# The opening stage's inputs loaded up front, its repeated query terms written by the engines and stored in one piece

## Chip, cores, metric

One NeuronCore of a Trainium2 chip. The metric is the device time of one launch in microseconds. TensorE multiplies matrices into eight PSUM banks, ScalarE and VectorE work on rows of up to 128 partitions, GpSimd has little to do here, and SyncE issues every DMA. Sixteen DMA engines carry the transfers.

## What is computed

Two transformer layers over x of shape 8 x 512 x 128, 16 heads of width 8: attention with learned relative positions (layer 0), a gated mixing layer, attention with a relative shift (layer 1), and a gated dense layer, each followed by a residual and a layer norm. The change touches only what comes ahead of the first attention:

```
Q = heads(x @ Wq.T + bq);  K = heads(x @ Wk.T + bk);  V = heads(x @ Wv.T + bv)
pos_key   = heads(rel_emb @ Wpk.T + bpk)
pos_query = heads(rel_emb @ Wpq.T + bpq)
scores = (Q K^T + take(Q pos_key^T, rel_pos) + take(K pos_query^T, p2c_pos)^T) * scale
```

## The kernel before

The kernel runs in five stages with a barrier between them: `opening_phase`, `attention_phase(0)`, `mixing_phase`, `attention_phase(1)`, `dense_phase`. A stage's semaphores are raised one by one at its start (`start_phase`, L77) and cleared one by one at its end (`end_phase`, L85). The opening stage has 59 of them, the attention stage after it 46. There is no planner: each engine has its program written out in order, and semaphores join them.

**What the opening stage makes.** Scores are formed later in bf16 at nearly fp32 precision. For that each value is split into three bf16 parts, high, middle and low, and a product becomes six terms: the queries' part follows `Q_PART = [0, 0, 0, 1, 1, 2]` and the keys' part `K_PART = [0, 1, 2, 0, 1, 0]`. `TERM_RUNS = [(0, 3, 0), (3, 2, 1), (5, 1, 2)]` lists runs of equal query parts: first term, length, part. The stage writes to DRAM, for each of eight batches b: `stack[0][b, 0]` (keys, 128 channels x 6 terms x 512 positions in bf16, 786,432 B), `stack[0][b, 1]` (queries, the same size), `values` (294,912 B), `offsets` (64 rows x 3 parts x 512, 196,608 B; its DRAM order is `h a k t` and the store walks it as `a h (k t)`, with a of size 4 outermost), and once the `table` of position differences (16 heads x 48 rows x 256 in bf16, in pieces of 256 B).

**SyncE (L161 to L246)** loads `xt` for batch 0, the weights (L195 to L200) and `xt` for batch 1, then waits until VectorE has set its blank buffers, writes zeros to `shear_a` and `shear_b` (L206, L209), ones into `stks` (L212), and goes through its loop over b: `values` (L167); for b < 6 a wait until the offset product of batch b has been made, and the load of `xt` for b + 2 into the buffer that this frees (L163); six stores of the stack in pieces of 3, 2 and 1 terms, keys (L173) and queries (L176, which read the same 1 KB row n times); `offsets` of b - 1 (L180); for b < 3 four of twelve table stores (L185, L186); for b = 3 the first loads of the attention stage (tables and offsets, L232 to L235); for b > 3 the first heads' loads (L190, L191). It ends with the last offsets store and waits for all of it.

**TensorE (L248 to L290)**: for each batch the query product (L253), the key product (L255), four value products (L261), and, two batches behind, the offset product (L266), which reads `xt` last.

**ScalarE**: for each batch `queries_keys` (L296, L299, PSUM to `full`), `high` (L306, one cast of keys and queries, 1024 columns, into `part`, after the stack stores of b - 2), `offset_high` (L315, L319, after the offsets store of b - 2), `middle` (L310, 1024 columns) and `offset_middle` (L323).

**VectorE**: `values_set` (L353), `remainder` (L360, `full` minus high), `offset_remainder` (L369), `low` (L364, remainder minus middle), `offset_low` (L373). The buffers `xt`, `full`, `left`, `part`, `off`, `off_left`, `off_part` and `vt` are pairs, used by b % 2.

Of the kernel before, what the change touches and what calls it, by code (L numbers as in the profile page):

```python
# [22 lines left out]
H = 16  # L23
# [40 lines left out]
def build(nc, t):  # L64

    top = ExitStack()
    with top:
# [45 lines left out]
        def opening_phase(stks, tabs, ident):  # L113

            with ExitStack() as ctx:
# [6 lines left out]
                def s(name):  # L122
                    return sem(f"o_{name}")
# [7 lines left out]
                dpart = [sb(f"dpart{i}", [C, 2, REL], BF16) for i in range(3)]  # L131
# [4 lines left out]
                xt = pair("xt", [C, T])  # L136
                full, left, part = pair("full", [C, 2, T]), pair("left", [C, 2, T]), pair("part", [C, 2, 3, T], BF16)
                off, off_left, off_part = pair("off", [4 * H, T]), pair("off_left", [4 * H, T]), pair("off_part", [4 * H, 3, T], BF16)
# [6 lines left out]
                x_in = [s(f"x_in{i}") for i in range(2)]  # L145
# [8 lines left out]
                N_STACK = 2 * len(TERM_RUNS)  # L154
# [4 lines left out]
                with nc.Block() as block:  # L159
                    @block.sync  # L160
                    def _(sp):  # L161
                        def load_x(b):
                            sp.dma_start(xt[b % 2][:, :], t["xT"][b]).then_inc(x_in[b % 2], 16)  # L163
# [6 lines left out]
                        def write_stack(b):  # L170
                            sp.wait_ge(lo_set, BASE + b + 1)
                            for first, n, q in TERM_RUNS:
                                sp.dma_start(stack[0][b, 0, :, first:first + n, :].rearrange("c j t -> c (j t)"),  # L173
                                             part[b % 2][:, 0, 0:n, :].rearrange("c j t -> c (j t)")).then_inc(stack_out[b], 16)
                                same = bass.AP(part[b % 2][:, :, :, :].tensor, (3 + q) * T, [[6 * T, C], [0, n], [1, T]])
                                sp.dma_start(stack[0][b, 1, :, first:first + n, :], same).then_inc(stack_out[b], 16)  # L176

                        def write_offsets(b):
                            sp.wait_ge(off_lo, BASE + b + 1)
                            sp.dma_start(offsets[b].rearrange("h a k t -> a h (k t)"),  # L180
                                         off_part[b % 2][:, :, :].rearrange("p k t -> p (k t)")).then_inc(off_out[b], 16)
# [19 lines left out]
                        load_x(1)  # L201
# [11 lines left out]
                        for b in range(B):  # L213
                            write_values(b)
                            if b + 2 < B:
                                sp.wait_ge(off_mm, BASE + b + 1)
                                load_x(b + 2)
# [3 lines left out]
                            if b < 3:  # L221
                                if b == 0:
                                    sp.wait_ge(dsplit, BASE + 4)
                                for j in (2 * b, 2 * b + 1):
                                    write_table(j)
                            if b == 3:
                                sp.wait_ge(stack_out[0], BASE + 16 * N_STACK)
                                sp.wait_ge(off_out[0], BASE + 16)
                                sp.wait_ge(table_out, BASE + 16 * 2 * NTERM)
# [19 lines left out]
                    def _(pe):  # L249
                        def project(b):  # L250
                            pe.wait_ge(x_in[b % 2], BASE + 16 * (b // 2) + 16)
                            pe.wait_ge(q_set, BASE + b - 1)
                            pe.matmul(q_bank[b % 2][:, :], wq[:, :], xt[b % 2][:, :], start=True, stop=True).then_inc(q_mm, 1)  # L253
                            pe.wait_ge(k_set, BASE + b - 1)
                            pe.matmul(k_bank[b % 2][:, :], wk[:, :], xt[b % 2][:, :], start=True, stop=True).then_inc(k_mm, 1)  # L255
# [3 lines left out]
                            for n in range(NT):  # L259
                                q = slice(128 * n, 128 * n + 128)  # L260
                                last = pe.matmul(v_bank[b % 2][:, q], xt[b % 2][:, q], wv[:, :], start=True, stop=True)  # L261
                            last.then_inc(v_mm, 1)

                        def offset_product(b):
                            pe.wait_ge(off_set, BASE + b)
                            pe.matmul(off_bank[0:4 * H, :], w_off[:, :], xt[b % 2][:, :], start=True, stop=True).then_inc(off_mm, 1)  # L266
# [1516 lines left out]
```

## Time and profile before

| | |
|---|---|
| median of 3 runs | 2092.57 us (2091.52 to 2100.56) |
| profiled execution | 2092.16 us |
| its span | 2090.0 us, mean granted TensorE clock 0.937 |
| TensorE busy | 1741.7 us, 83% of the span |
| ScalarE busy | 1476.3 us, 71% |
| VectorE busy | 1447.2 us, 69% |
| DMA | 432,880 packets, 404.38 MB |
| opening stage | up to 103.0 us, and 7.28 us to the first instruction of the attention |

A row of the profile names the line, the engine, the operation and the tiles (out<-in). PE is TensorE's matmul, PEld its weight load, ACT ScalarE, DVE VectorE, SPq SyncE's queue as it issues transfers; an SPq row's length is the time of the issue, not of the transfer. Times count from the start of the span. The DMA share is the mean busy share of the sixteen DMA engines; packets that overlap can take it a little over 1.

### The profile page before, as it was taken

The page shows a single profiled execution, that of the slowest core. Times are in us where ns is not written, and L with a number is a line of the kernel's source. Part 1 is how long each engine was busy: PE and PEld are TensorE (multiplying, and loading weights), DVE is VectorE, ACT ScalarE, POOL GpSimd, SP SyncE. Part 2 cuts the span into 40 slices and gives each one's busy share as a digit, 9 for nine tenths or more (in the row PEclk, how much of TensorE's full clock was granted, in tenths as well). Part 3 has the DMA queues.
Part 4 walks back from the last instruction along what each step waited for, and adds up shares of the span by engine and source line. Part 5 has one row for each costly group of instructions (what it writes and reads, how often), then busy time and mean ns, then how long its engine had stood idle before and what let it go on. Part 6 is the DMA issues. An engine that isn't in the chain of part 4 may idle for free. (4 is left out here: it accounts for less than half of the span.)

```text
span 2090.0 us, 44501 instructions
## 1 busy us (share of the span) xinstructions
PE 1741.7 (83%) x11694; PEld 1049.1 (50%) x11694; DVE 1447.2 (69%) x3484; ACT 1476.3 (71%) x2600; POOL 79.7 (4%) x102
## 2 busy tenths in 40 slices
PE   5359999889898988874760899999999994999998
PEld 3135555555555555543540555656655652545544
DVE  5348888878888888854982888889888882324422
ACT  4338888888888888863871899999999992223222
POOL 0000000000000000001530000000000000000000
PEclk8659999999999999996985899999999997999999
DMA  6758888888888888846787777777777763100100
GB/s 192 240 169 258 253 255 253 261 245 253 257 258 255 254 245 253 255 124 170 249 300 232 199 215 213 211 211 213 214 211 214 211 164 101 35 20 25 35 5 10
DMA packets 432880, 404.38 MB, mean 193 GB/s; under 512 B 38522, under 2 KB 354098, under 8 KB 432690
## 3 DMA queue, kind: packets, MB, share of 16 engines
q1 hardware_dynamic: 432817, 403.66, 66.1%
q8 instruction: 26, 0.43, 0.1%
q14 instruction: 37, 0.30, 0.0%
HBM read 227.09 MB, written 175.77 MB: 193 GB/s over the span
## 5 line engine op out<-in xcount | busy, mean ns | idle before, releaser
L891 ACT ACTIVATE a_prob<-bank,a_negmax 128x512 f32<-128x512 f32 x1024 | 733.5, 716 | 81.6 <-DVE a_negmax L828 79.7
L828 DVE TENSOR_REDUCE a_negmax<-bank 128x1 f32<-128x512 f32 x1024 | 699.1, 683 | 0.1
L711 PE MATMUL bank<-a_ident,a_prob 128*128 128x128 f32 x4096 | 645.1, 280 | 53.2 <-ACT a_probt L898 43.9
L898 ACT COPY a_probt<-bank 128x512 f32<-128x512 f32 x1024 | 615.7, 602 | 82.4 <-PE bank L711 69.0
L711 PEld LDWEIGHTS bank<-a_ident,a_prob 128*128 128x128 f32 x4096 | 449.9, 141 | 172.9 <-ACT a_probt L898 69.1
L820 DVE TENSOR_TENSOR bank<-bank,a_band 128x128 f32<-128x128 f32 (+3 forms) x1024 | 350.5, 342 | 123.4 <-PE bank L692 68.9
L690 PE MATMUL bank<-a_stks 74*128 74x192 bf16 (+7 forms) x1024 | 324.4, 317 | 10.0 <-ACT a_prob L891 9.8
L724 PE MATMUL bank<-a_probt,a_vs 128*32 128x512 f32 x2048 | 273.9, 609 | 15.0 <-ACT a_probt L898 15.0
L690 PEld LDWEIGHTS bank<-a_stks 74*128 74x128 bf16 (+1 forms) x1024 | 100.3, 98 | 233.2 <-ACT a_prob L891 204.6
L808 DVE COPY_PREDICATED bank<-a_mask,bank 128x128 f32<-128x128 uint32 (+1 forms) x512 | 139.3, 272 | 90.7 <-PE bank L696 90.6
L692 PE MATMUL bank<-a_stks 74*128 74x320 bf16 (+5 forms) x768 | 200.9, 262 | 0.0
L696 PE MATMUL bank<-a_stks 74*128 74x128 bf16 (+1 forms) x512 | 111.2, 217 | 41.0 <-DVE bank L808 31.9
L1660 DVE TENSOR_TENSOR d_drop<-bank,d_s 128x128 f32<-128x128 f32 x32 | 7.1, 283 | 170.5 <-PE bank L1583 170.5
L738 PE MATMUL bank<-a_ident,a_sheared 128*128 128x128 f32 x512 | 105.9, 284 | 12.7 <-DMA a_sheared<-shear_a 12.5
L1562 PE MATMUL bank<-d_ha,d_h1T 128*128 128x512 f32 x256 | 112.3, 592 | 0.0
L1562 PE MATMUL bank<-d_hb,d_h2T 128*128 128x512 f32 x256 | 111.2, 592 | 0.0
L909 ACT COPY a_corr<-bank 128x512 f32<-128x512 f32 x128 | 76.2, 595 | 39.0 <-PE bank L739 38.9
L833 DVE COPY a_corr<-bank 128x512 f32<-128x512 f32 x128 | 87.1, 681 | 17.7 <-PE bank L748 10.4
L838 DVE COPY a_keyside<-bank 128x512 f32<-128x512 f32 x128 | 87.2, 682 | 16.8 <-PE bank L731 13.6
L696 PEld LDWEIGHTS bank<-a_stks 74*128 74x128 bf16 x512 | 49.7, 97 | 97.1 <-DVE bank L808 88.3
L739 PE MATMUL bank<-a_tabs,a_stks 65*128 65x128 bf16 x512 | 97.0, 224 | 0.0
L748 PE MATMUL bank<-edges,a_stks 96*128 96x128 bf16 x512 | 51.0, 223 | 52.8 <-DMA a_ident<-in_ident 45.2
(176 smaller groups left out, 1568.9 us busy)
## 6 DMA issues: line engine op xcount, KB each, us to landing
a_band<-shear_b SPq DMA_DIRECT2D x128, 512.0 KB, 4.3
shear_a<-a_keyside SPq DMA_DIRECT2D x128, 256.0 KB, 3.3
a_sheared<-shear_a SPq DMA_DIRECT2D x128, 256.0 KB, 3.9
shear_b<-a_corr SPq DMA_DIRECT2D x128, 256.0 KB, 4.7
shear_e<-a_corr SPq DMA_DIRECT2D x128, 256.0 KB, 2.3
a_band<-shear_e SPq DMA_DIRECT2D x128, 256.0 KB, 3.3
a_stks<-stack SPq DMA_DIRECT2D x256, 96.0 KB, 2.5
a_stks<-stack SPq DMA_DIRECT2D x384, 48.0 KB, 2.6
```

Source lines behind the costliest of these rows:

```text
L690: last = pe.matmul(score[:, 0:c], k[:, qlo, q], k[:, keys, 0:c], start=True, stop=True)
L692: last = pe.matmul(score[:, c:T], k[:, qhi, q], k[:, keys, c:T], start=True, stop=True)
L696: last = pe.matmul(other[:, 0:e - a], k[:, qhi, q], k[:, keys, a:e], start=True, stop=True)
L711: last = pe.transpose(turned_bank[k][:, n * 128:(n + 1) * 128], prob[h.slot % 2][:, n, k * 128:(k + 1) * 128], ident[:, :])
L724: pe.matmul(cbank[32 * j:32 * j + VW, :], vs[g][:, at:at + VW], probt[h.slot + j][:, k, :], start=(k == 0), stop=(k == NT - 1)).then_inc(p ...
L738: pe.matmul(corr_bank[:, q], sheared[h.slot % 4][:, q], ident[:, :], is_transpose=True, start=True, stop=False)
L808: v.copy_predicated(score[:, a:e], mask[:, 0:e - a], other[:, 0:e - a]).then_inc(fixed, 1)
L820: v.tensor_tensor(score[:, a:e], score[:, a:e], band[h.slot % bands][:, n, w:w + e - a], ALU.add).then_inc(added, 1)
L828: v.tensor_reduce(negmax[h.slot % 2][:, n:n + 1], score[:, :], AX.X, ALU.max, negate=True).then_inc(maxed, 1)
L891: nc.scalar.activation(prob[h.slot % 2][:, n, :], score[:, :], ACT.Exp, bias=negmax[h.slot % 2][:, n:n + 1]).then_inc(exped, 1)
L898: nc.scalar.copy(probt[h.slot][:, k, :], turned_bank[k][:, :]).then_inc(copied, 1)
L1562: last = pe.matmul(dst[:, :], w[:, k, 128 * m:128 * m + 128], src[:, k, :], start=(k == 0), stop=(k == KH - 1))
```

## The change

- All eight `xt` have a buffer and a semaphore of their own (`x_in` becomes eight semaphores) and are loaded ahead of SyncE's wait for the blank buffers. The wait for the offset product and the load inside SyncE's loop are gone.
- `part` becomes one tensor of nine rows of 512: rows 0 to 2 are the keys' parts, rows 3 to 8 the queries' six terms as they stand in DRAM. `high` on ScalarE is two casts: 512 columns of the keys, and the queries' 512 columns written three times (1536). `middle` moves to VectorE and is two casts, 512 columns and 512 written twice. `remainder` and `low` read and write through strided views.
- A stack is stored by four transfers, not six: the queries in one piece (6 KB a partition), then the keys in three.
- `off_part` has three buffers, not two.
- `dpart` is one tensor, and the tables are stored by six transfers, not twelve, of two or more pieces of 256 B each where a run has more than one term.

```diff
-                x_in = [s(f"x_in{i}") for i in range(2)]
+                x_in = [s(f"x_in{b}") for b in range(B)]
...
                         def write_stack(b):
                             sp.wait_ge(lo_set, BASE + b + 1)
+                            sp.dma_start(stack[0][b, 1].rearrange("c j t -> c (j t)"),
+                                         part[b % 2][:, 3:, :].rearrange("c j t -> c (j t)")).then_inc(stack_out[b], 16)
                             for first, n, q in TERM_RUNS:
                                 sp.dma_start(stack[0][b, 0, :, first:first + n, :].rearrange("c j t -> c (j t)"),
-                                             part[b % 2][:, 0, 0:n, :].rearrange("c j t -> c (j t)")).then_inc(stack_out[b], 16)
-                                same = bass.AP(part[b % 2][:, :, :, :].tensor, (3 + q) * T, [[6 * T, C], [0, n], [1, T]])
-                                sp.dma_start(stack[0][b, 1, :, first:first + n, :], same).then_inc(stack_out[b], 16)
+                                             part[b % 2][:, 0:n, :].rearrange("c j t -> c (j t)")).then_inc(stack_out[b], 16)
...
-                        def write_table(j):
-                            rows = table[:, :, :].rearrange("h (c j) r -> h c j r", j=NTERM)[:, :, j, :]
-                            sp.dma_start(rows[:, :, 0:REL], dpart[Q_PART[j]][:, 0, :]).then_inc(table_out, 16)
-                            sp.dma_start(rows[:, :, REL:2 * REL], dpart[K_PART[j]][:, 1, :]).then_inc(table_out, 16)
+                        def write_table(first, n, q):
+                            rows = table.rearrange("h (c j) r -> (h c) j r", j=NTERM)[:, first:first + n, :]
+                            same = bass.AP(dpart[:, :, :, :].tensor, q * REL, [[6 * REL, C], [0, n], [1, REL]])
+                            sp.dma_start(rows[:, :, 0:REL], same).then_inc(table_out, 16)
+                            sp.dma_start(rows[:, :, REL:2 * REL], dpart[:, 1, 0:n, :]).then_inc(table_out, 16)
...
-                        load_x(1)
+                        for b in range(1, B):
+                            load_x(b)
                         sp.wait_ge(blank, BASE + N_BLANK)
...
                             write_values(b)
-                            if b + 2 < B:
-                                sp.wait_ge(off_mm, BASE + b + 1)
-                                load_x(b + 2)
                             write_stack(b)
...
-                                for j in (2 * b, 2 * b + 1):
-                                    write_table(j)
+                                write_table(*TERM_RUNS[b])
...
-                            nc.scalar.copy(part[b % 2][:, :, 0, :], full[b % 2][:, :, :]).then_inc(hi_set, 1)
-
-                        def middle(b):
-                            act.wait_ge(rest, BASE + b + 1)
-                            nc.scalar.copy(part[b % 2][:, :, 1, :], left[b % 2][:, :, :]).then_inc(mid_set, 1)
+                            nc.scalar.copy(part[b % 2][:, 0, :], full[b % 2][:, 0, :])
+                            nc.scalar.copy(part[b % 2][:, 3:6, :], bass.AP(full[b % 2][:, :, :].tensor, T, [[2 * T, C], [0, 3], [1, T]])).then_inc(hi_set, 1)
...
+                        def middle(b):
+                            v.wait_ge(rest, BASE + b + 1)
+                            v.tensor_copy(part[b % 2][:, 1, :], left[b % 2][:, 0, :])
+                            v.tensor_copy(part[b % 2][:, 6:8, :], bass.AP(left[b % 2][:, :, :].tensor, T, [[2 * T, C], [0, 2], [1, T]])).then_inc(mid_set, 1)
...
                             values_set(b)
                             remainder(b)
+                            middle(b)
                             offset_remainder(b - 1)
                             low(b)
                             offset_low(b - 1)
```

## Rows read from the trace of the kernel before

**Rows 1.** The page, part 1: busy us (share of the span) and instructions.

```profile
PE 1741.7 (83%) x11694; PEld 1049.1 (50%) x11694; DVE 1447.2 (69%) x3484; ACT 1476.3 (71%) x2600; POOL 79.7 (4%) x102
```

**Rows 2.** Windows: us; busy PE, PEld, DVE, ACT, POOL; clock; DMA share; GB/s.

```profile
10.00:14.00 4.00, 4.00 (x14) 2.67 (x13) 2.63 (x4) 1.47 (x3) 0.00 (x0) 1.00 0.38 110
20.00:22.00 2.00, 0.00 (x0) 0.00 (x0) 1.90 (x6) 1.97 (x3) 0.00 (x0) 0.64 0.18 31
34.00:35.00 1.00, 0.15 (x1) 0.15 (x1) 0.78 (x1) 0.70 (x2) 0.00 (x0) 0.61 1.04 416
35.00:38.00 3.00, 3.00 (x4) 1.37 (x5) 1.04 (x2) 0.69 (x1) 0.00 (x0) 0.50 1.07 381
20.11:103.00 82.89, 38.80 (x86) 18.86 (x86) 32.84 (x41) 36.47 (x50) 0.00 (x0) 0.69 0.74 240
81.65:90.84 9.19, 2.19 (x4) 0.25 (x3) 4.20 (x5) 3.35 (x5) 0.00 (x0) 0.87 0.78 255
88.00:91.00 3.00, 0.00 (x0) 0.00 (x0) 0.00 (x0) 0.00 (x0) 0.00 (x0) 0.64 0.38 107
100.00:103.00 3.00, 0.00 (x0) 0.00 (x0) 0.00 (x0) 0.00 (x0) 0.00 (x0) 0.50 0.26 97
103.00:110.28 7.28, 0.00 (x0) 0.00 (x0) 0.00 (x0) 0.00 (x0) 0.00 (x0) 0.50 0.00 1
```

**Rows 3.** Timeline at the stage's two edges: start us, us, engine, line, operation.

```profile
4.41 0.42 SPq L163 DMA_DIRECT2D o_xt<-in_xT  x1
...
110.28 0.11 DVE L843 MEMSET a_vs<- 128x23 f32 x2 [14.91 <-PEq L77]
```

**Rows 4.** Table of waits, first 110 us: us in total, times, longest us.

```profile
PE bank L253 <- DMA o_xt<-in_xT: 25.6, 6, 6.0
...
ACT o_off_part L319 <- DMA offsets<-o_off_part: 8.3, 3, 6.5
```

**Rows 5.** SyncE's own waits, first 103 us.

```profile
SPq L163 <- PE bank L266: 3.8, 3, 2.5
```

**Rows 6.** Timeline of one turn of the `xt` loop.

```profile
31.90 0.34 SPq L163 DMA_DIRECT2D o_xt<-in_xT  x1
...
34.85 2.08 PE L253 MATMUL bank<-o_xt,o_wq 128*128 128x512 f32 x2 [2.98 <-DMA o_xt<-in_xT]
...
41.75 0.34 SPq L163 DMA_DIRECT2D o_xt<-in_xT  x1
```

**Rows 7.** Instructions on tile `o_part`: duration ns min/median/max, first and last start.

```profile
L173 SPq DMA_DIRECT2D stack<-o_part x24: 432/790/1198, 22.2 to 94.8; - x24
```

**Rows 8.** Timeline, SyncE late in the stage.

```profile
89.02 1.31 SPq L190 DMA_DIRECT2D a_stks<-stack  x1
...
98.31 1.14 SPq L180 DMA_DIRECT2D offsets<-o_off_part  x1
```

**Rows 9.** Timeline, start of the fills, of batch 1 and of the loop.

```profile
12.98 0.94 SPq L206 DMA_DIRECT2D shear_a<-o_zf  x2
...
18.60 0.68 ACT L296 ACTIVATE o_full<-bank,o_bqs 128x512 f32<-128x512 f32 x1
...
20.11 1.26 SPq L167 DMA_DIRECT2D values<-o_vt  x1
```

**Rows 10.** ScalarE by line and shape, whole span: busy us, mean ns.

```profile
L1221 ACT CAST m_part<-m_full 128x1538 bf16<-128x1538 f32 x8 | 11.9, 1489 | 4.1 <-DMA stack<-m_part 4.1
...
L296 ACT ACTIVATE o_full<-bank,o_bqs 128x512 f32<-128x512 f32 x8 | 5.5, 686 | 18.3 <-PE bank L253 18.3
...
L319 ACT CAST o_off_part<-o_off 64x512 bf16<-64x512 f32 x8 | 4.9, 617 | 8.5 <-DMA offsets<-o_off_part 8.3
```

**Rows 11.** VectorE by line and shape, whole span.

```profile
L360 DVE TENSOR_TENSOR o_left<-o_full,o_part 128x1024 f32<-128x1024 f32 x8 | 9.7, 1218 | 1.4 <-ACT o_part L306 1.4
...
L369 DVE TENSOR_TENSOR o_off_left<-o_off,o_off_part 64x512 f32<-64x512 f32 x8 | 5.5, 683 | 11.3 <-ACT o_off_part L319 11.3
...
L1670 DVE COPY d_x<-d_x1n 128x512 f32<-128x512 f32 x8 | 3.2, 398 | 0.1
```

More of the change, by code:

```diff
@@ L130, in opening_phase @@
                 diff, drest = sb("diff", [C, 2, REL]), sb("drest", [C, 2, REL])
-                dpart = [sb(f"dpart{i}", [C, 2, REL], BF16) for i in range(3)]
+                dpart = sb("dpart", [C, 2, 3, REL], BF16)
                 ends_k, ends_q = sb("ends_k", [C, 2 * H]), sb("ends_q", [C, 2 * H])
@@ L135, in opening_phase @@
                 zf, ones = sb("zf", [128, REL]), sb("ones", [3, T], BF16)
-                xt = pair("xt", [C, T])
-                full, left, part = pair("full", [C, 2, T]), pair("left", [C, 2, T]), pair("part", [C, 2, 3, T], BF16)
-                off, off_left, off_part = pair("off", [4 * H, T]), pair("off_left", [4 * H, T]), pair("off_part", [4 * H, 3, T], BF16)
+                xt = [sb(f"xt{b}", [C, T]) for b in range(B)]
+                full, left, part = pair("full", [C, 2, T]), pair("left", [C, 2, T]), pair("part", [C, 3 + NTERM, T], BF16)
+                hi_of, mid_of, lo_of = (lambda p: p[:, 0:4:3, :]), (lambda p: p[:, 1:7:5, :]), (lambda p: p[:, 2:9:6, :])
+                off, off_left = pair("off", [4 * H, T]), pair("off_left", [4 * H, T])
+                off_part = [sb(f"off_part{i}", [4 * H, 3, T], BF16) for i in range(3)]
                 vt = pair("vt", [128, H, NT, VC])
@@ L260, in project @@
                                 q = slice(128 * n, 128 * n + 128)
-                                last = pe.matmul(v_bank[b % 2][:, q], xt[b % 2][:, q], wv[:, :], start=True, stop=True)
+                                last = pe.matmul(v_bank[b % 2][:, q], xt[b][:, q], wv[:, :], start=True, stop=True)
                             last.then_inc(v_mm, 1)
@@ L316, in offset_high @@
                             act.wait_ge(off_set, BASE + b + 1)
[L317 to L319 removed]
+                            if b > 2:
+                                act.wait_ge(off_out[b - 3], BASE + 16)
+                            nc.scalar.copy(off_part[b % 3][:, 0, :], off[b % 2][:, :]).then_inc(off_hi, 1)
                         def offset_middle(b):
                             act.wait_ge(off_rest, BASE + b + 1)
[L323 removed]
+                            nc.scalar.copy(off_part[b % 3][:, 1, :], off_left[b % 2][:, :]).then_inc(off_mid, 1)
                         act.wait_ge(q_in, BASE + 64)
@@ L335, in _ @@
                         high(0)
-                        middle(0)
                         act.wait_ge(w_off_set, BASE + 2)
@@ L341, in _ @@
                             offset_high(b - 1)
-                            middle(b)
                             offset_middle(b - 1)
@@ L359, in remainder @@
                             v.wait_ge(lo_set, BASE + b - 1)
-                            v.tensor_tensor(left[b % 2][:, :, :], full[b % 2][:, :, :], part[b % 2][:, :, 0, :], ALU.subtract).then_inc(rest, 1)
+                            v.tensor_tensor(left[b % 2][:, :, :], full[b % 2][:, :, :], hi_of(part[b % 2]), ALU.subtract).then_inc(rest, 1)
+                        def middle(b):
+                            v.wait_ge(rest, BASE + b + 1)
+                            v.tensor_copy(part[b % 2][:, 1, :], left[b % 2][:, 0, :])
+                            v.tensor_copy(part[b % 2][:, 6:8, :], bass.AP(left[b % 2][:, :, :].tensor, T, [[2 * T, C], [0, 2], [1, T]])).then_inc(mid_set, 1)
                         def low(b):
                             v.wait_ge(mid_set, BASE + b + 1)
-                            v.tensor_tensor(part[b % 2][:, :, 2, :], left[b % 2][:, :, :], part[b % 2][:, :, 1, :], ALU.subtract).then_inc(lo_set, 1)
+                            v.tensor_tensor(lo_of(part[b % 2]), left[b % 2][:, :, :], mid_of(part[b % 2]), ALU.subtract).then_inc(lo_set, 1)
                         def offset_remainder(b):
```

33 lines of the change are left out of this document (15 added, 18 removed).

## The prediction

> **What bounds the kernel now.** I read the page first: over the whole span TensorE is the fullest engine [rows 1], but the change touches the opening stage alone, so only the stretch up to the attention stage counts. The opening's last packets land by 103.0; then 7.28 us pass with every engine and DMA idle, and the attention's first instruction starts at 110.28 [rows 2, 3]. From the first `values` store at 20.11 to 103.0 no engine is busy even half of the time (TensorE 38.8 of 82.9 us, ScalarE 36.5), and the DMA engines are busy 0.74 of it [rows 2]. The table of waits shows what the engines wait for: TensorE for `xt` 25.6 us in six waits [rows 4]. The timeline of one turn shows the loop: SyncE issues the load of `xt` at 31.90, its product starts at 34.85, and SyncE, which holds the next load until the offset product has read the buffer, issues that at 41.75 [rows 6]: 2.95 us for the load, 6.90 for the products, 9.85 us a turn.
>
> So the obvious reading is that the load's wait costs all this idle time. SyncE's own queue speaks otherwise. It waits for the offset product only 3.8 us, in three waits [rows 5]; for the rest it issues one transfer behind the other until 99.45 [rows 8]. An issue costs 0.42 us on an idle queue [rows 3], but the 24 issues of the stack's first kind cost 0.79 us in the median and up to 1.20 [rows 7], and a head's load 1.31 [rows 8]: transfers under way push the issues back. In the turn from 81.65 to 90.84 (between two `values` issues) no `xt` is loaded or waited for, and it still takes 9.19 us [rows 2]. Taking the load's wait away can't make a turn shorter than that queue needs, and DMA lies just under it.
>
> **What the transfers need.** While stacks are stored, the DMA engines are at 1.04 to 1.07 and move 381 to 416 GB/s [rows 2]; a batch's stack is 12 x 131,072 B = 1.57 MB, 4.1 us. From 100 to 103 only the last offsets store runs, and the busy share is 0.26 at 97 GB/s [rows 2]: a quarter of the engines carry it. Its 196,608 B take 2.0 us, while twelve engines idle and all that is queued behind waits for the four. The Trainium skill states why (page "DMA: Bandwidth & Descriptors", section "Rules for kernel authors"): the slowest dimension bounds how many engines a transfer gets, here 4; by that rule the trace agrees. The change leaves this store as it is.
>
> **The change, part by part.**
>
> 1. *The six `xt` loads of batches 2 to 7 leave the loop.* The three waits go: 3.8 us [rows 5]. The data of a load goes too: 262,144 B at about 400 GB/s [rows 2] is 0.65 us, 3.9 us for six; their issues lie inside that, since data pushes the queue back. Off SyncE's path: 7.7 us.
>
> 2. *They come back ahead of the zero fills.* SyncE's fills start at 12.98 [rows 9]; six more issues of 0.42 us or little more put that at 14.6 or later. The DMA share is only 0.38 from 10 to 14 [rows 2], so some of the data is hidden, about 1.1 us after the first added load. Of 3.9 us of data 2.8 us are left, and the fills, the ones and the first `values` store (20.11 [rows 9]) move by that, to 22.9. Bounds: 1.6 us (about the issues' own time beyond the slack of SyncE's wait for the memsets) to 3.9 us (nothing hidden). Queued behind it: `values` 0, stack 0, the tables. The engines lose nothing: batch 0's products need only what was issued before.
>
> 3. *Queries stored in one piece.* Three stores that read 1 KB again and again become one with 6 KB a partition; the bytes are the same. Nearest rows: 416 GB/s in a stack store's first us (`xt` in rows of 2 KB, the keys' first piece in 3 KB) and 381 after that, keys and queries mixed [rows 2]. Half a stack at 416 in place of 381 is 1.89 in place of 2.06 us; with two transfers fewer I take 0.3 us a batch, 2.4 us in all. Bounds: nothing, if only bytes count; two issues of 0.8 us a batch [rows 7], if issues do (the first rival).
>
> 4. *Tables in six transfers, not twelve.* The same pieces of 256 B. I take 0.5 us. Bounds: nothing, to six issues of 0.8 us, 4.8 us.
>
> 5. *ScalarE writes the queries' high part three times, VectorE takes the middle parts.* High becomes 0.62 (512 columns) and 1.49 us (by the cast of 1538 columns), 2.11 us [rows 10]. The middle casts of 512 and 1024 columns are taken at the copy of 512, 0.40, and twice that, 1.2 us; at the rate of the two-operand form (1.22 for 1024) they are 1.8 us [rows 11]. The loop that joins the two engines (queries and keys, high, remainder, middle, the offsets' remainder, their middle on ScalarE, next batch) is then 1.37 + 2.11 + 1.22 + 1.20 + 0.68 + 0.62 = 7.2 us [rows 10, 11], with some 0.1 us between steps 7.7; 8.3 with slow casts. SyncE's turns of 8.4 us and more, below, cover it, so I cost it at nothing. Were the cover gone, it would set the end: batch 1 starts at 18.6 [rows 9], six more turns, 8.2 us to the last low part, and 12.2 us as now from the last `values` issue (90.84) to 103.0: 39.0 + 6 x 7.7 = 85.2 us, or 88.8 with slow casts.
>
> 6. *A third `off_part`.* ScalarE's 8.3 us of waits for the offsets' stores [rows 4] go or shrink. The last offsets store is issued at 98.31, behind a head's loads [rows 8], not late for its data: nothing.
>
> 7. *Six more semaphores.* 59 become 65. They are raised before the first load at 4.41 [rows 3], 0.07 us each; the 7.28 us after 103.0 hold 59 clears and the 46 raises of the next stage, 0.07 us again [rows 2]. Twelve more steps: +0.84 us on the path.
>
> Sum: -7.7 + 2.8 - 2.4 - 0.5 + 0.84 = -7.0 us. In time: 22.9, then 82.9 - 7.7 - 2.4 - 0.5 = 72.3 us, ends at 95.2 instead of 103.0. The profiled execution took 2092.16 us, 2.2 us around its span of 2090.0, and lies 0.4 us under the runs' median of 2092.57, so one base serves for both: 2092.2 - 7.0 = **2085.2 us**. Late next is SyncE's queue again, pushed back by the stacks and the four engines of the offsets.
>
> **The rivals.**
>
> *Transfers count, not bytes.* If SyncE is pushed back because only so many transfers may be under way, each one removed gives its issue back: 16 stack issues of 0.8 us are 12.8 us, six of the tables 4.8. For it: from 88 to 91, among the heads' small loads, the DMA share is only 0.38 [rows 2] and an issue still takes 1.31 us [rows 8]. Against it: in a stack's 5 us the DMA engines are full. The end is then set by the four busiest of them. From 20.11 to 103 the mean is 0.74 x 82.9 = 61.3 us; the offsets need 8 x 2.0 us there but count a quarter in the mean, +12; less 3.9 for `xt`, and divided by the 1.05 that a full engine shows, 66 us. From 22.9 that ends at 89: -14 + 0.84, **2079 us**. The Trainium skill rules this way (same page and section): coalesce many small transfers into a large one. By it the sum would be this rival's; no row here parts its rule from the byte count.
>
> *The loads are hidden anyway.* Waits and data of `xt` go (7.7 us), the moved loads cost their whole 3.9 us, and one large store gains nothing: -7.7 + 3.9 + 0.84, **2089 us**. For it: bytes stay, and DMA is full during stacks. Against it: from 20 to 22, behind the fills, DMA is busy 0.18 [rows 2] and SyncE is pushed back all the same (1.26 us for `values` [rows 9]), so bytes are not all.
>
> *The one large store lands on few engines*, as the offsets do. At 97 GB/s its 786 KB take 8.1 us in place of 2.06: 6.0 us in each of eight batches, 48 us, **2133 us**. For it: the offsets do so in this trace [rows 2]. Against it: the keys' stores have the same form, 128 partitions outermost, and all engines are full in them. It makes the kernel slower from 2.3 us a batch on, with the store at 4.4 us, under 180 GB/s.
>
> **How the numbers follow.** Forecast 0.55, counting 0.28, hidden 0.13, few engines 0.04. About 0.5%, 10.5 us, is what a measurement of this kernel can tell from no change. Under 2082.1 lies nearly all of counting and about a seventh of the forecast (it needs 3 us more, issues given back for part): faster 0.35. Slower 0.04, within 0.61. The forecast's own terms (start, stack, tables) span 2081 to 2089. The range takes in both near rivals: 2078 to 2090.
>
> **What would show it.** In the profile after: the first `values` issue near 22.9; no wait of TensorE for `xt`; turns of SyncE of 8.4 to 8.9 us, stack issues still well over 0.43 us; the last packet near 95. If turns are near 7.7 us and issues short, counting was right and the loop of ScalarE and VectorE takes over. If the query store takes over 4 us at a low share, it sits on few engines. The prediction is wrong if SyncE's queue is free after the change, or if what follows 110.28 takes another time than now.

## The result: 1.6% slower, by something outside the changed stage

The kernel after takes 2129.27 us (median of 4 runs, 2126.97 to 2131.63), the kernel before 2095.52 us beside it (4 runs, 2091.52 to 2100.56): a ratio of 1.0159, with a 95% interval of 1.0141 to 1.0177. The forecast of 2085.2 us was wrong by 44 us, and on the wrong side.

The opening stage itself took the time that was forecast, though not by the terms that were forecast (below). The timeline of after at its edges and around SyncE's loop (start us, us, engine, line, operation):

```profile
4.76 0.41 SPq L165 DMA_DIRECT2D o_xt<-in_xT  x1
...
12.62 2.33 SPq L165 DMA_DIRECT2D o_xt<-in_xT  x5
14.99 0.98 SPq L210 DMA_DIRECT2D shear_a<-o_zf  x2
...
23.25 1.15 SPq L169 DMA_DIRECT2D values<-o_vt  x1
...
102.66 0.11 DVE L845 MEMSET a_vs<- 128x23 f32 x2 [21.04 <-PEq L77]
```

The attention's first instruction comes at 102.66, not at 110.28 [rows 3]: 7.62 us earlier, where the sum said 7.0. The loop starts at 23.25 (forecast 22.9; 20.11 before [rows 9]); the last packets land between 94.5 and 95 (forecast 95). Yet the span grew from 2090.0 to 2126.2 us. The page of after, its parts 1 to 3 (the share of each engine; GB/s in 40 slices of the span; the queues that fetch instructions):

```profile
span 2126.2 us, 44506 instructions
...
PE 1754.9 (83%) x11694; PEld 1051.3 (49%) x11694; DVE 1454.3 (68%) x3500; ACT 1478.9 (70%) x2600; POOL 79.7 (4%) x102
...
GB/s 237 189 208 247 256 249 251 248 258 258 256 251 251 255 247 256 249 78 180 324 311 175 204 194 190 192 194 195 198 189 194 210 190 99 35 20 20 39 5 10
...
q14 instruction: 77, 0.63, 0.1%
```

and the same two lines of the page of before:

```profile
GB/s 192 240 169 258 253 255 253 261 245 253 257 258 255 254 245 253 255 124 170 249 300 232 199 215 213 211 211 213 214 211 214 211 164 101 35 20 25 35 5 10
...
q14 instruction: 37, 0.30, 0.0%
```

The engines have hardly more work than before [rows 1]: VectorE runs 16 instructions more, and TensorE is busy 13.2 us longer with the same 11694 (its clock, below); the rest of the 36 us is idle time. Two things differ. In slices 24 to 31, in the second attention (`attention_phase(1)`), DMA moves 189 to 198 GB/s instead of 211 to 215. And queue q14, one of the two that bring instructions, has 77 packets instead of 37. The view of DMA over 1240 to 1640, inside that attention's loop, puts the two together. After:

```profile
q1 hardware_dynamic: 113543, 78.06, 70.5%
q14 instruction: 32, 0.26, 0.2%
```

Before, in the same window, the view has no q14 line at all:

```profile
q1 hardware_dynamic: 123294, 84.80, 75.9%
```

The timeline of after shows what such a fetch does; these are rows of SyncE and of who waits for it:

```profile
1228.75 0.36 SPq L589 DMA_DIRECT2D a_vs<-values  x1
1228.84 0.68 DVE L835 COPY a_corr<-bank 128x512 f32<-128x512 f32 x1
...
1234.12 0.39 SPq L574 DMA_DIRECT2D shear_e<-a_corr  x1
...
1234.92 0.38 SPq L581 DMA_DIRECT2D a_band<-shear_e  x1
...
1238.43 0.30 DVE L822 TENSOR_TENSOR bank<-bank,a_band 128x128 f32<-128x128 f32 x1 [3.95 <-DMA a_band<-shear_e]
...
1239.35 0.69 ACT L893 ACTIVATE a_prob<-bank,a_negmax 128x512 f32<-128x512 f32 x1 [3.44 <-DVE a_negmax L830]
...
1240.09 0.39 PE L692 MATMUL bank<-a_stks 96*128 96x512 bf16 x1 [3.30 <-ACT a_prob L893]
```

and the same place in before:

```profile
1233.36 0.37 SPq L587 DMA_DIRECT2D a_vs<-values  x1
1233.42 0.68 DVE L833 COPY a_corr<-bank 128x512 f32<-128x512 f32 x1
...
1234.35 0.38 SPq L572 DMA_DIRECT2D shear_e<-a_corr  x1
```

In before, `a_corr` is there at 1233.42 + 0.68 = 1234.10, and SyncE issues its store 0.25 us later. In after it is there at 1229.52, and SyncE issues at 1234.12, 4.6 us later. What lies ahead of that issue in SyncE's program is the branch from the loop's end to its start, at 1229.24: the next issue comes 4.9 us after the branch, and 4.7 to 5.1 us after it in all eight turns, where it is 0.5 us in before. The trace has instruction fetches on q14 at 1230.3, 1232.5 and 1234.7, each of 8 KB, and two more before the next turn, at 1260.0 and 1283.8. Then the three engines wait in a row: VectorE for the band that `shear_e` brings, ScalarE for VectorE, TensorE for ScalarE. The table of waits over 1180 to 1750 has that wait once in before, and ten times in after:

```profile
DVE bank L820 <- DMA a_band<-shear_e: 0.5, 1, 0.5
```

```profile
DVE bank L822 <- DMA a_band<-shear_e: 31.9, 10, 4.2
```

**The balance of the span.** SyncE's loop of this stage is 288 instructions long and is passed nine times, with eight branches back. A turn is counted from the end of one pass to the end of the next.

| stretch | before | after | difference |
|---|---|---|---|
| to the attention's first instruction | 110.28 | 102.66 | -7.6 |
| from there to the end of the loop's first pass | 1123.6 | 1126.6 | +3.0 |
| eight turns | 8 x 54.0 = 431.9 | 8 x 59.0 = 472.0 | +40.1 |
| from the end of the ninth pass to the end | 424.3 | 425.0 | +0.7 |
| span | 2090.0 | 2126.2 | +36.2 |

The +3.0 ahead of the loop is within the scatter: in the profiled executions of the 14 kernels of this document that stretch takes 1119.3 to 1130.6 us.

**The theory.** Instructions come in pieces of 8 KB. In the part of a turn of after where no branch lies between, SyncE runs 122 to 134 instructions from one fetch to the next, so a piece is taken as 128. What SyncE holds is a few pieces. The loop of 288 instructions touches three pieces if it starts at most 96 instructions behind an edge, and four otherwise. With three it stays, and nothing is fetched for 400 us, as before. With four, and one more that is fetched ahead, pieces are thrown out before the branch needs them again, and each turn fetches five anew. The change never touched that loop; it made SyncE's program ahead of it 10 instructions shorter, and so moved the loop over an edge.

The rivals: the new work itself slows the attention (how the opening leaves memory, or the two extra buffers); or the total number of instructions does, whatever their place; or TensorE's granted clock, whose mean is 0.927 in after and 0.937 in before.

### The profile page after: what moved, and what is told of

Same layout as the page of the kernel before. It is cut to its first block and busy times, and to the rows that moved or that the text cites. A ratio compares the mean times of both kernels' runs of the same rounds, so it can differ in the third digit from the quotient of the medians.

```text
span 2126.2 us, 44506 instructions
## 1 busy us (share of the span) xinstructions
PE 1754.9 (83%) x11694; PEld 1051.3 (49%) x11694; DVE 1454.3 (68%) x3500; ACT 1478.9 (70%) x2600; POOL 79.7 (4%) x102
## 5 line engine op out<-in xcount | busy, mean ns | idle before, releaser
L713 PEld LDWEIGHTS bank<-a_ident,a_prob 128*128 128x128 f32 x4096 | 454.8, 143 | 173.1 <-ACT a_probt L900 69.6
L726 PE MATMUL bank<-a_probt,a_vs 128*32 128x512 f32 x2048 | 281.5, 624 | 15.2 <-ACT a_probt L900 15.2
L840 DVE COPY a_keyside<-bank 128x512 f32<-128x512 f32 x128 | 87.3, 682 | 16.6 <-PE bank L733 13.2
```

The costliest lines, as they stand in the source:

```text
L713: last = pe.transpose(turned_bank[k][:, n * 128:(n + 1) * 128], prob[h.slot % 2][:, n, k * 128:(k + 1) * 128], ident[:, :])
L726: pe.matmul(cbank[32 * j:32 * j + VW, :], vs[g][:, at:at + VW], probt[h.slot + j][:, k, :], start=(k == 0), stop=(k == NT - 1)).then_inc(p ...
```

## Experiments on the cause

**Move the loop, change nothing else.** Sixteen raises of a semaphore that nobody waits for any more, in SyncE's queue ahead of its last waits of the opening stage:

```diff
                             write_offsets(B - 1)
+                        for _ in range(16):
+                            sp.sem_inc(blank, 1)
```

> The changed kernel with 16 more semaphore raises on SyncE, behind its last offsets store, where it waits for landings anyway. Two theories on the 44 us that the profile after shows behind the opening stage. Fetch: SyncE's program became shorter by 10 instructions up to the loop of attention_phase(1), and that loop of 288 instructions now lies across one more 8 KB piece of instructions than before, so that it is fetched anew in each of nine turns (5 us of standstill a turn). 16 more instructions put it back behind the edge: the 44 us go, the opening's gain of 7.6 us stays, so about 2129.3 - 44 = 2085 us, ratio to the kernel before about 0.996, and no instruction fetches on queue 14 between 1230 and 1640 us. Rival, something else of the change (VectorE's 16 added instructions, other SBUF addresses, the clock): SyncE's raises change nothing, 2129 us, ratio 1.016, five fetches a turn stay.

Measured: 2085.68 us, ratio 0.9972 [0.9959, 0.9985]; a turn is 54.0 us, and no q14 packet falls into 1240 to 1640; the mean granted clock is 0.938. The first attention instruction is at 103.15. So the changed kernel with 16 useless instructions more is 44 us faster than without, and faster than before.

**The counter-test: before, without the change, moved the other way.** The semaphores `v_out` become two for eight, so SyncE's program ahead of the loop is 12 instructions shorter (the waits for them, not shown, count up accordingly):

```diff
-                v_out, stack_out, off_out = ([s(f"{n}{b}") for b in range(B)] for n in ("v_out", "stack_out", "off_out"))
+                v_out = [s(f"v_out{i}") for i in range(2)] * (B // 2)
+                stack_out, off_out = ([s(f"{n}{b}") for b in range(B)] for n in ("stack_out", "off_out"))
```

> The kernel before with two semaphores for the values stores instead of eight: nothing else changes, SyncE has 12 instructions fewer ahead of the loops (six raises, six clears), and less to do. Fetch: the loop of attention_phase(1) moves across the edge as it did in the changed kernel (that was 10 fewer), nine turns lose 4 to 5 us: ratio 1.017 to 1.022, about 2130 to 2138 us, with five fetches of 8 KB a turn. Rival: 0.8 us faster at most, ratio 0.9996.

Measured: 2133.46 us, ratio 1.0204 [1.0173, 1.0236], a turn 58.9 us. In the view of DMA over 1240 to 1640 and in the table of waits over 1180 to 1750 the kernel of before now looks like after:

```profile
q14 instruction: 32, 0.26, 0.2%
```

```profile
DVE bank L821 <- DMA a_band<-shear_e: 32.3, 10, 4.7
```

None of the change is in this kernel, so the new work isn't needed for the loss: that rival falls. The number of instructions is not settled by this kernel, for it has fewer than before, as after has. It falls with two others: after_pad128 (next) has 118 more than before ahead of the loop and loses, and fewer_semaphores (below) has 63 fewer and doesn't.

**A whole piece more, and a control.** The same edit on after with 128 raises puts the loop one piece further, at the same distance from an edge as in after; the same 16 raises on before leave it among three pieces.

> The changed kernel with 128 raises in the same place, one whole 8 KB piece of instructions (between two fetches SyncE runs through 122 to 134 instructions in the profile after). Fetch: the loop lies over the edges just as in the changed kernel, so the 44 us stay and the raises cost 128 x 0.07 = 9 us less the 2 to 3 us that the last landing hides: 2129 + 6 = 2135 us, ratio 1.019. If any added length cured it, not the place in the piece, it would be 2085 + 6 = 2091 us, ratio 0.998. The rival (nothing to do with fetches) gives 2135 too, but then after_pad16 stays at 2129.

> Control: the kernel before with the same 16 raises. Both theories: the loop stays clear of the edge, the raises hide behind the last offsets store's landing, ratio 1.000 within 0.001, up to 1 us longer. If the padding itself gained something, this would show it.

Measured: 2129.73 us, ratio 1.0179 [1.0154, 1.0204], turns of 59.05 us; and 2093.05 us, ratio 1.0007 [0.999, 1.0024], turns of 53.9 us. The loss comes back after 128 instructions, and 16 raises cost nothing by themselves. In after_pad128 the attention also starts 6 us later than in after_pad16, at 109.31, for the raises stand on the path there.

**The upper edge.** Till here "the loop must not start just ahead of an edge" would do as a rule. The theory says more: it also fails when the loop starts well behind an edge but its end crosses into a fourth piece. With 102 raises it starts some 100 instructions behind an edge:

> The changed kernel with 102 raises, to find the other edge. Pieces of instructions hold 128 (between fetches SyncE runs 122 to 134), the loop has 288, so it lies in three pieces only if it starts in the first 96 of one. In the changed kernel it starts one instruction ahead of an edge; 102 raises let it start 101 behind it and end 5 behind the third. By the number of pieces the loss is back: turns of 58 to 59 us, five fetches a turn (four with the loop, one ahead), ratio about 1.018. If what hurt was only that the loop's start lay just ahead of an edge, turns stay at 54 us and the ratio is 0.999.

Measured: 2117.21 us (4 runs, 2103.93 to 2122.11; before there 2088.24), ratio 1.0142 [1.0116, 1.0168]. Five fetches a turn again, and in the window 1240 to 1640:

```profile
q1 hardware_dynamic: 117617, 80.94, 73.6%
q14 instruction: 35, 0.29, 0.2%
```

The rule by pieces holds: four pieces, five fetches a turn. The size does not: the profiled execution, which is the fastest of the four (its span is 2102.1 us), loses only 56.5 - 54.0 = 2.5 us a turn. There SyncE issues the load of `values` at 1280.64 and the next `shear_e` at 1284.19, 3.55 us apart instead of 5.4 as in after.

**What a turn's loss is made of.** The turns of after_pad102 aren't alike, and TensorE's granted clock tells them apart. Four of its eight turns (window: us; busy PE, PEld, DVE, ACT, POOL; clock; DMA share; GB/s):

```profile
1338.03:1393.73 55.70, 50.85 (x428) 32.29 (x420) 47.34 (x109) 53.06 (x100) 0.00 (x0) 1.00 0.75 206
1393.73:1450.87 57.14, 52.37 (x428) 33.04 (x420) 47.45 (x109) 53.17 (x100) 0.00 (x0) 0.97 0.73 201
1450.87:1506.69 55.82, 50.84 (x428) 32.28 (x420) 47.35 (x109) 53.07 (x100) 0.00 (x0) 1.00 0.75 205
1506.69:1564.24 57.55, 52.41 (x428) 32.80 (x420) 47.44 (x109) 53.17 (x100) 0.00 (x0) 0.97 0.72 199
```

The four turns at 1.00 take 55.7 to 56.1 us, the four at 0.97 take 56.9 to 57.6, some 1.3 us more. In after the clock falls in every turn, for longer in two of them, and in before's turns it doesn't. A turn of before, two turns of after, and the fall itself, in after's first turn:

```profile
1233.85:1287.71 53.86, 50.67 (x424) 32.26 (x420) 47.51 (x109) 52.87 (x100) 0.00 (x0) 1.00 0.75 212
```

```profile
1229.24:1288.26 59.02, 52.43 (x424) 32.80 (x421) 47.46 (x109) 53.19 (x100) 0.00 (x0) 0.97 0.70 195
1288.26:1348.07 59.81, 53.36 (x424) 33.74 (x420) 47.52 (x109) 53.27 (x100) 0.00 (x0) 0.94 0.69 192
1240.70:1244.10 3.40, 3.40 (x15) 1.31 (x16) 1.60 (x4) 2.54 (x5) 0.00 (x0) 0.50 0.83 238
```

In that last window TensorE, which has just stood idle for 3.30 us up to 1240.09, works at the lower of its two levels (1.2 instead of 2.4 GHz). So the clock is no rival to the fetches but follows from them: in this loop it falls behind the standstill, and not in turns in which nothing is fetched. By these rows an estimate for a turn of after is 3.7 us of standstill and 1.3 us of lower clock. That also says why after_pad102 loses less: SyncE issues the load of the band that VectorE waits for 3.8 to 4.0 us after the branch there, 5.5 to 5.9 in after (1.2 in before, 5.2 to 6.0 in the other two slow kernels), and half of its turns keep the full clock. Its four executions go with the clock too (2103.93 us at a mean of 0.939, 2112.99 at 0.934, 2121.43 at 0.930, 2122.11 at 0.931). But four turns more at the lower clock are only some 5 us of the 18 between them; why the rest varies, and why the standstill is shorter, stays open.

**All kernels side by side.** How far the loop is moved against before, in instructions that SyncE ran ahead of it, and the length of a turn:

| moved by | turn, us | kernel |
|---|---|---|
| -63 | 53.9 | fewer_semaphores |
| -12 | 58.9 | before_sems6_fewer |
| -10 | 59.0 | after |
| 0 | 54.0 | before |
| +1 | 53.9 | combined |
| +6 | 54.0 | after_pad16 |
| +6 | 53.9 | two_off_part |
| +12 | 53.9 | tables_twelve |
| +16 | 53.9 | before_pad16 |
| +22 | 53.9 | queries_three_pieces |
| +28 | 54.0 | loads_only |
| +30 | 53.9 | offsets_four_stores |
| +92 | 56.5 | after_pad102 |
| +118 | 59.1 | after_pad128 |

With pieces of 128 and 3 of them held, all fourteen rows fit if before's loop starts 5 to 9 instructions behind an edge: -10 must fall short of it (at most 9), +92 must take the start more than 96 behind an edge (at least 5). The edge's place is fitted to these rows; no view shows it. The Trainium skill (page "Runtime: NRT & Kernel Launch", section "Instruction fetch mechanics") says that instructions are refilled in blocks of 256 and that a taken branch to a place outside the window of two blocks forces a fetch before work goes on. The traces agree that the branch forces it. With blocks of 256, though, a loop of 288 moved by +92 or +118 would lie in two blocks, as it does unmoved (for -10 and -12 to lose, before's loop would have to start at most 9 behind an edge of such blocks), and these two kernels lose all the same: here it is pieces of 8 KB, and the measurement decides.

## Experiments on the opening stage

With the loop put back where it stays, the terms of the sum can be told apart. Each kernel is read by its profile: when the attention's first instruction comes. That moment moves a little by itself: 110.28 in before, 109.03 with 16 raises; 102.66 in after, 103.15 with 16 raises and 102.92 with another edit of no effect (below). So a term under some 1.3 us can't be settled by one profile of each.

**The loads alone.** before with eight `xt`, all loaded ahead of the fills, and the 16 raises:

```diff
-                        load_x(1)
+                        for b in range(1, B):
+                            load_x(b)
...
-                            if b + 2 < B:
-                                sp.wait_ge(off_mm, BASE + b + 1)
-                                load_x(b + 2)
```

> The kernel before with all eight inputs loaded ahead of the fills and nothing else of the change (16 raises behind the last offsets store keep the later loop in its place). It sizes the first two terms of the sum. Mine: 7.7 us off SyncE's path, 2.8 us back at the start, 0.84 us for six semaphores and about 0.5 us for the raises: the attention's first instruction at 110.28 - 3.6 = 106.7 us, no wait of TensorE for xt. Rival, the load's wait was the whole bound: the gain of the full change (7.1 us in the stage) is here already, 103.2 us.

Measured: 2091.28 us, ratio 0.9992 [0.9975, 1.0009]; the attention starts at 108.80, 1.5 us earlier than in before and only 0.2 us earlier than in before with 16 raises. The loop starts at 23.84, 3.7 us later, and its last `values` is issued at 88.61, so the seven turns take 64.8 us instead of 70.7: 6.0 us less (7.7 forecast). Neither expectation holds, neither 106.7 nor 103.2. TensorE doesn't wait for `xt` any more, but ScalarE does for the stores; the table of waits of loads_only, first 110 us:

```profile
ACT o_part L306 <- DMA stack<-o_part: 21.8, 6, 6.4
...
ACT o_off_part L319 <- DMA offsets<-o_off_part: 14.1, 6, 6.6
```

In before they were 1.0 us and 8.3 us (the latter in [rows 4]). The 25.6 us of waiting for the load moved, nearly whole, to the waiting for buffers of the stores: the transfers set the pace.

**Queries in three pieces.** after_pad16, with the queries' six terms written by the engines as in after, but stored by three transfers:

```diff
-                             sp.dma_start(stack[0][b, 1].rearrange("c j t -> c (j t)"),
-                                          part[b % 2][:, 3:, :].rearrange("c j t -> c (j t)")).then_inc(stack_out[b], 16)
                             for first, n, q in TERM_RUNS:
+                                sp.dma_start(stack[0][b, 1, :, first:first + n, :].rearrange("c j t -> c (j t)"),
+                                             part[b % 2][:, 3 + first:3 + first + n, :].rearrange("c j t -> c (j t)")).then_inc(stack_out[b], 16)
```

> after_pad16 with the queries stored in three pieces of 3, 2 and 1 KB a partition instead of one of 6 KB: same bytes, two transfers more in each batch. Bytes (my forecast, 0.3 us a batch): the attention starts up to 2.4 us later than the 103.15 us of after_pad16, at 103.2 to 105.6. Transfers count (0.8 us an issue): 12.8 us later, 116 us.

Measured: 2086.67 us, ratio 0.9975 [0.9958, 0.9991]; attention at 104.50, 1.35 us later than after_pad16, for 16 transfers more of the same bytes: 0.08 us each, just at the limit of what one profile can tell, and far from the 0.8 of the counting rival. The instructions on `o_part`, in after_pad16 and then in this kernel (duration in ns: min/median/max), show why:

```profile
L177 SPq DMA_DIRECT2D stack<-o_part x24: 428/1211/1261, 25.5 to 86.5; - x24
L174 SPq DMA_DIRECT2D stack<-o_part x8: 502/506/2110, 24.7 to 84.2; - x8
```

```profile
L175 SPq DMA_DIRECT2D stack<-o_part x24: 459/706/1798, 25.2 to 88.3; - x24
L177 SPq DMA_DIRECT2D stack<-o_part x24: 439/645/1092, 26.0 to 89.0; - x24
```

With four transfers a batch the keys' issues take 1.21 us, with six 0.65 (the last line). By the medians that is 24 x 1.211 + 8 x 0.506 = 33.1 us of issuing against 24 x (0.706 + 0.645) = 32.4 us: fewer issues, each pushed back longer, until the bytes are away.

**Tables in twelve transfers.** after_pad16 with before's loop over single terms:

```diff
-                                write_table(*TERM_RUNS[b])
+                                for j in (2 * b, 2 * b + 1):
+                                    write_table(j)
```

> after_pad16 with the tables stored by twelve transfers as before. I had priced six fewer at 0.5 us; the turns of batches 0 to 2 lie 3.4 us closer together with six (queries_three_pieces against loads_only). If the tables' transfers are that difference, the attention starts about 3 us later than at 103.15, near 106; if it comes from the engines' order, it stays within 0.5 us of 103.15.

Measured: 2088.12 us, ratio 0.9979 [0.9961, 0.9998]; attention at 105.63, 2.5 us later than after_pad16. Six transfers fewer are worth 0.4 us each, five times what the stack's are. These are pieces of 256 B, the stack's of 1 KB and more; that this is the reason isn't shown.

**Two `off_part` again.** after_pad16 with the third buffer taken back:

```diff
-                off_part = [sb(f"off_part{i}", [4 * H, 3, T], BF16) for i in range(3)]
+                off_part = pair("off_part", [4 * H, 3, T], BF16)
```

> after_pad16 with two off_part buffers instead of three, so that ScalarE waits for the offsets store of b - 2 again (8.3 us of such waits in the kernel before). My step 6: nothing, attention from 103 us on. Rival: ScalarE is now close enough to the bound for this to reach SyncE, up to 0.9 us in each of the last batches, 104 to 106 us.

Measured: 2088.66 us, ratio 0.9982 [0.9963, 1.0002]; attention at 102.92, as without the edit. ScalarE waits 6.6 us for the offsets again, and it changes nothing.

**The offsets by four transfers.** after_pad16, one transfer for each of the four outer rows, of 16 partitions:

```diff
-                             sp.dma_start(offsets[b].rearrange("h a k t -> a h (k t)"),
-                                          off_part[b % 3][:, :, :].rearrange("p k t -> p (k t)")).then_inc(off_out[b], 16)
+                            for k in range(4):
+                                sp.dma_start(offsets[b, :, k].rearrange("h k t -> h (k t)"),
+                                             off_part[b % 3][H * k:H * k + H, :, :].rearrange("p k t -> p (k t)")).then_inc(off_out[b], 16)
```

> after_pad16 with the offsets stored by four transfers of 16 partitions each, heads outermost, instead of one whose outermost size is 4. If four DMA engines are the bound of a turn (196,608 B in 2.0 us on a quarter of the engines, 0.5 us on all), up to 1.5 us a batch go, 12 us: attention from 91 us on. If transfers count, three more a batch cost 24 x 0.6 = 14 us: 117 us. If only bytes count and the queue hides the four engines: 103 us. In the last 3 us of the stage the DMA share should no longer stand at 0.25.

Measured: 2082.53 us, ratio 0.996 [0.9938, 0.9983]; attention at 100.74, 2.4 us earlier, with 24 transfers more. From 89 to 92, the end of the stage's transfers, the DMA share is 0.50, where in before the last offsets store alone ran at 0.26 [rows 2]. The store on four engines does cost something, but a fifth of the 12 us that it would if the four were the bound.

**Fewer semaphores.** after with 3 semaphores for `x_in`, 2 each for `v_out` and `stack_out`, 3 for `off_out`, and the last waits for those alone, 22 semaphores and 17 waits less (shown in part):

```diff
-                x_in = [s(f"x_in{b}") for b in range(B)]
+                x_in = [s(f"x_in{i}") for i in range(3)]
...
-                v_out, stack_out, off_out = ([s(f"{n}{b}") for b in range(B)] for n in ("v_out", "stack_out", "off_out"))
+                v_out, stack_out, off_out = ([s(f"{n}{b % r}") for b in range(B)] for n, r in (("v_out", 2), ("stack_out", 2), ("off_out", 3)))
```

> The changed kernel with 22 semaphores fewer in the opening stage (three for xt instead of eight, two for values, two for stacks, three for offsets) and 7 final waits in place of 24. 44 raises and clears at 0.07 us are 3.1 us, the waits 0.5 to 1 us. SyncE's program is 53 instructions shorter than in the changed kernel, which puts the loop of attention_phase(1) well inside three pieces, with no padding. Fetch theory: no fetches in that loop, attention from 99.5 us on, about 2086 - 3.5 = 2082 us, ratio 0.9955. If the place was not the cause, it stays at 1.016.

Measured: 2082.31 us, ratio 0.9951 [0.9935, 0.9968]; attention at 100.15, 2.5 us earlier than in after, 3.0 than with 16 raises. At 0.07 us for a raise and a clear, 44 x 0.07 = 3.1 us. This kernel has no padding: its loop, moved by -63, lies in three pieces again.

**All of it together.** fewer_semaphores, the offsets in four transfers, one semaphore for fills, tables and first loads, and 44 raises that keep the loop in place (moved by +1):

> fewer_semaphores with the offsets in four stores of 16 partitions and one semaphore for fills, tables and first loads; 44 raises behind the last store keep the later loop 6 instructions above the edge. Attention from 103.15 - 3.0 (semaphores) - 2.4 (offsets) = 97.7 us on if the two gains add, no later than 100 if they overlap; in all about 2079.5 us, ratio 0.994. Were the edge misjudged, 2124 us.

Measured: 2083.58 us (12 runs), ratio 0.9947 [0.9928, 0.9965]; attention at 97.81, 12.5 us earlier than in before, and the loop starts at 22.62. It is the earliest attention of all, but the whole kernel is no faster than fewer_semaphores within the intervals: between the profiled executions of the 14 kernels the stretch from the attention's first instruction to the end of the loop's first pass varies by 11 us, more than these edits bring.

## Why the prediction was wrong, by its own steps

- **The step that failed: one base for everything after 110.28.** The sum stopped at the stage's end and added 2092.2. Its last sentence named the case ("what follows 110.28 takes another time than now") but gave it neither a mechanism, nor a price, nor a chance. It is where the whole error lies: +40.1 us in eight turns of a loop that the diff doesn't touch, because SyncE's instructions for it are fetched anew in each turn. With the loop back in place the same change gives 2085.68 us, the forecast's number, though beside a before of 2091.59: 5.9 us gained, where the sum said 7.0.
- **What was missing in the working** is a count of SyncE's instructions as code, not as time. Step 7 counted instructions (twelve steps of 0.07 us), and step 1 counted issues that move; no step added up that the program ahead of the second attention becomes 10 instructions shorter. The view that bore on it was read for bytes only: part 3 of the page of before, with 37 packets of q14 in the whole span. So few say that the attention loops aren't fetched again, and that they could begin to be.
- **The loads** (-7.7 + 2.8, with 0.84 for the semaphores: -4.1): the mechanism was right, for both the turns (-6.0) and the start (+3.7) moved as said, but both sizes were off the same way, to a net of -0.2 to -1.5 us. The second rival, hidden anyway, had the moved loads right (3.9 us), but it too took the whole 7.7 off the turns.
- **The queries** (-2.4, bounds 0 and two issues of 0.8 a batch): -1.35 for the two transfers fewer. Nearer to "only bytes count". The rival of counting is refuted here: issues of 1.21 us in place of 0.79 [rows 7] ate what fewer issues gave.
- **The tables** (-0.5, bounds 0 to -4.8): -2.5. Under-sized. They come nearer to the rival of counting (0.8 each) than the stack does, at half of it.
- **The casts on ScalarE and VectorE** (at nothing): high takes 0.62 + 1.47 us, middle 0.42 + 0.68 us, both as taken, the lower figure for the middle. SyncE's first two turns, of 7.0 and 7.7 us, are about as short as the two engines' own loop; from the third on they are 8.4, 10.6, 8.6, 8.6 and 8.4 us. In all seven turns SyncE waits for VectorE only twice, 0.7 and 1.1 us, so the cover held but for that. The first two turns were not the 8.4 us and more that the step counted on.
- **`off_part`** (nothing) was right, and **the semaphores** (0.07 us each) nearly: the first load comes 0.35 us later for six more, and 22 fewer of them, with 17 waits, gave 2.5 to 3.0 us.
- **The large store on few engines**: refuted. It is issued in 0.50 us in the median, and the turn from 74.03 to 82.47 runs at a DMA share of 0.79 and 278 GB/s.
- The sum of -7.0 against -7.6 is thus partly luck: of the 7.6 us from before to after (5.9 between the two with 16 raises) the parts measured alone give 5.4 (4.1 with the loads against before_pad16). The rest, some 2 us, isn't assigned. What is left for it is that the same 1 KB of the queries is no longer read again and again, that the middle casts changed engines, and the scatter of about 1 us between profiles; none was tried alone.

## What to carry to other kernels

Where an engine runs a loop, an edit anywhere ahead of it in that engine's program moves the loop against the pieces in which its instructions are fetched, and can cost more than the edit is worth: here 40 us for 10 instructions less. So compare the packets of the instruction queues and the length of a loop's turn between the two pages before explaining a difference by the edit; a few idle instructions that move the loop are the test, and also the cure. Look at the granted clock of the turns too: here a stretch at half the clock follows each standstill of after, for an estimated 1.3 of the 5.0 us. And where issues are pushed back, cost a transfer by its bytes if its pieces are large, and expect the next ones to take back what one issue less gives.

## What the runs showed of the hardware beyond that

- Queue q14 brings instructions in pieces of 8 KB. By the 14 kernels, SyncE's loop of 288 instructions isn't fetched again (no q14 packet from 1240 to 1640 in before) if it lies in three of them; in four it costs five fetches a turn, and 5.0 us a turn (2.5 us in the profiled execution of after_pad102).
- Behind a branch to a piece that is gone SyncE's next issue comes after 4.7 to 5.1 us in after, 3.0 to 3.2 in after_pad102 and 2.7 to 3.4 in before_sems6_fewer, against 0.5 in before, with fetches some 2.2 us apart in after.
- TensorE's granted clock falls to half in every turn of after, for the first time at 1240.7, behind 3.30 us of idling; a turn in which it falls is some 1.3 us longer in after_pad102.
- Raises in SyncE's queue behind its last transfer cost 0.03 to 0.05 us each, part of it hidden by the last landing: against after's 102.66, 16 of them put the attention at 103.15, 102 at 106.04 and 128 at 109.31.
- Four transfers of 49,152 B, each from 16 partitions, in place of one of 196,608 B on a quarter of the engines gave 2.4 us in eight batches.
